# New positions for the chains' pieces of a two-layer kernel on four engines, with the transfers of SyncE left where they are

## The reference

```python
def step(h, inp):                                  # the scan: 512 channels x 16 states x 1024 positions, 4 batches
    a, bx, c = inp
    h = a * h + bx                                 # a = exp(dt * A), bx = dt * B_t * x_branch
    y = jnp.einsum('bds,bs->bd', h, c)
    return (h, y)
def step(c, xt):                                   # the recurrence over the 4 batches
    ft = jax.nn.sigmoid(xt @ wf.T + c @ uf.T + bf)
    it = jax.nn.sigmoid(xt @ wi.T + c @ ui.T + bi)
    gt = jnp.tanh(xt @ wc.T + c @ uc.T + bc)
    c = ft * c + it * gt
```

## Time and profile before

| | |
|---|---|
| time, median of 3 runs | 1270.59 us (1269.78 to 1272.22) |
| the profiled execution | 1271.65 us, of which the span is 1270.1 us |
| VectorE busy | 1159.2 us, 91% |
| TensorE busy | 1145.3 us, 90% |
| GpSimd busy | 980.9 us, 77% |
| ScalarE busy | 794.3 us, 63% |
| mean granted TensorE clock | 0.984 |

### The profile page before, as it was taken

How to read it: one execution, slowest core, us unless ns; L and a number is a source line. 1 busy time by engine, 2 the same in 40 slices (tenths; PEclk the granted TensorE clock), 3 DMA queues, 4 the chain that set the end, 5 groups by cost and what they waited for, 6 DMA issues and landing times.

```text
span 1270.1 us, 12563 instructions
## 1 busy us (share of the span) xinstructions
PE 1145.3 (90%) x3612; PEld 641.0 (50%) x3612; DVE 1159.2 (91%) x1136; ACT 794.3 (63%) x1443; POOL 980.9 (77%) x711
## 2 busy tenths in 40 slices
PE   7989678998999899998999899998999899889896
PEld 4636333654457444764457444764457444443454
DVE  3868999999999999899999999899999999999987
ACT  2256567765785677855786678855786666645522
POOL 3216886889788988989778888989778896876852
PEclk9999989999999999999999999999999999989999
DMA  8308588876878677876768588866868686989922
GB/s 280 118 15 301 188 268 286 275 233 234 278 234 291 214 275 276 296 233 235 279 219 302 207 276 286 290 230 239 281 228 292 204 279 222 306 314 351 369 84 99
DMA packets 92308, 313.87 MB, mean 247 GB/s; under 512 B 10432, under 2 KB 15680, under 8 KB 91984
## 3 DMA queue, kind: packets, MB, share of 16 engines
q1 hardware_dynamic: 89936, 306.26, 70.1%
q10 hardware_dynamic: 2304, 6.82, 1.6%
HBM read 301.73 MB, written 11.31 MB: 246 GB/s over the span
## 4 chain that ended last, share of the span: by engine, by line
PE 46%; DVE 19%; POOL 16%; ACT 9%; issue 8%; DMA 2%; SPq 0%; DVEq 0%; POOLq 0%; ACTq 0%
PE ps L874 14%; DVE ps L1691 11%; POOL arena L1914 9%; PE ps L585 5%; PE ps L808 4%; PE ps L593 3%; PE ps L631 2%; DVE arena L1697 2%; PE ps L707 2%; PE ps L720 2%; PE ps L712 2%; PE ps L735 2%; ACT arena L898 2%; ACT ps L1254 2%; PE ps L728 1%
## 5 line engine op out<-in xcount | busy, mean ns | idle before, releaser
L1914 POOL TENSOR_TENSOR arena<-arena 128x1024 f32<-128x1024 f32 x255 | 600.7, 2364 | 139.9 <-PE ps L874 115.2
L1691 DVE TENSOR_TENSOR_SCAN ps<-ps,arena 128x1024 f32<-128x1024 f32 (+1 forms) x257 | 585.9, 2280 | 29.6 <-ACT ps L1254 16.7
L874 PE MATMUL ps<-arena,identF 128*128 128x512 f32 x1024 | 484.0, 604 | 46.7 <-DVE arena L1697 29.7
L1254 ACT ACTIVATE ps<-arena,negA 128x512 f32<-128x512 f32 x512 | 332.8, 684 | 89.6 <-DVE arena L1697 83.9
L874 PEld LDWEIGHTS ps<-arena,identF 128*128 128x128 f32 x1024 | 190.8, 193 | 266.6 <-issue 209.5
L1697 DVE TENSOR_TENSOR arena<-ps,arena 128x1024 f32<-128x1024 f32 x256 | 312.0, 1219 | 5.9
L889 ACT ACTIVATE arena<-arena,rnln 128x256 f32<-128x256 f32 x118 | 61.9, 590 | 42.5 <-POOL rnln L1724 25.7
L631 PE MATMUL ps<-arena,inw 128*128 128x512 f32 x128 | 60.0, 614 | 11.7 <-ACT arena L898 9.6
L712 PE MATMUL ps<-arena,inw 128*128 128x512 f32 x128 | 62.0, 608 | 3.3 <-DVE arena L1421 3.3
L1266 ACT ACTIVATE arena<-ps 128x2 f32<-128x2 f32 x128 | 22.1, 172 | 67.9 <-DVE arena L1697 67.4
L898 ACT ACTIVATE arena<-ps,modT 128x512 f32<-128x512 f32 x43 | 51.7, 1264 | 13.7 <-PE ps L458 11.6
(11 more groups left out here) (219 smaller groups left out, 1715.7 us busy)
## 6 DMA issues: line engine op xcount, KB each, us to landing
arena<-bc_scratch SPq DMA_DIRECT2D x511, 512.0 KB, 5.0
arena<-in_x SPq DMA_DIRECT2D x16, 256.0 KB, 6.8
arena<-in_x SPq DMA_DIRECT2D x8, 512.0 KB, 8.9
xr_scratch<-arena SPq DMA_DIRECT2D x6, 512.0 KB, 6.7
px_scratch<-arena SPq DMA_DIRECT2D x6, 512.0 KB, 6.3
out_x<-arena SPq DMA_DIRECT2D x5, 512.0 KB, 2.6
arena<-bc_scratch SPq DMA_DIRECT2D x9, 256.0 KB, 3.7
woT<-in_woT SPq DMA_DIRECT2D x4, 512.0 KB, 9.4
```

The costliest lines, as they stand in the source:

```text
L874: x = pe.matmul(ps[:, Y, :], identF[:], inp[:, m % RING, q, :], start=False, stop=(i == BLOCK_STEPS - 1 and q == 1), skip_group_check=True)
L1254: x = act.activation(ps[:, 2 * (m % 2) + q, :], dt[:, kd, :], ACT.Exp, scale=negA[:, kd, 2 * i + q:2 * i + q + 1])
L1691: x = dve.tensor_tensor_scan(states, states, inp[:, m % RING, q, :].rearrange("p q t -> p (q t)"), 0.0, ALU.mult, ALU.add)
L1914: x = pool.tensor_tensor(inp[:, m % RING, :, :], u[:, kd:kd + 1, :].broadcast_to([P, 2, TH]), b_at[:, m % 3, :, :], ALU.mult)
```

## The change

All tables of `TIMES` for TensorE, ScalarE, VectorE and GpSimd get new numbers, most of them moved by a quarter of a step to two steps. The three tables of SyncE stay. No instruction is added or removed apart from ScalarE's loads of function tables, which follow the order. Lines of the difference that are spoken of below:

```diff
-    "pool_before": {"wo_gate": -5.75, "ffn_gate": -5.75, "ln1_rstd": -4.25, "ga_bias": 6.5, "op_add": (12, 12),
+    "pool_before": {"wo_gate": -7, "ffn_gate": -7, "ln1_rstd": -3.75, "ga_bias": 5.75, "op_add": (12, 12),
...
-        "first_decay": (35, 37.75), "softplus": (33.75, 34.25), "dt_copy": 37.75, "xc_silu": 28.5},
+        "first_decay": (35, 38), "softplus": (34.25, 34.25), "dt_copy": 38, "xc_silu": 27.75},
...
-        "softplus": (33.75, 33.75), "dt_copy": 41.25, "xc_silu": 28.5},
+        "first_decay": (35.75, 39), "softplus": (31.5, 34.25), "dt_copy": 39, "xc_silu": 28},
```

More of the change, by code:

```diff
@@ L67 @@
[L67 to L72, removed]
@@ L73 @@
-    "dve_second": {"ln1_stats": -13.5, "ln1_moments": -11.25, "smax": (6.75, 9), "rsum": (9, 9.5),
[3 rows of a table removed]
-    "pool_before": {"wo_gate": -5.75, "ffn_gate": -5.75, "ln1_rstd": -4.25, "ga_bias": 6.5, "op_add": (12, 12),
[L78 to L82, removed]
@@ L83 @@
-    "pool_after": {"cp_gate": -7.25, "cp_add": (5, 5), "ln4_rstd": 6.75, "f_c": 21, "i_g": 25.5, "c_new": 25.5},
[7 rows of a table added]
+        "gate_x": (12, 12.75, 17, 17.75, 21, 23.75), "gate_c": (12, 12.75, 17, 17.75, 21, 24.75), "px": (25.5, 26),
+        "om": 26},
+    "act_before": {"hn1": (-3.5, -3.5), "hB1": (-1.75, -1.75), "q0": -1.5, "k0": 1, "q1": 3.25, "exp0a": 3.75,
+        "exp0b": 3.75, "k1": 3.75, "v0": 7.25, "exp1a": 7.25, "exp1b": 7.25, "att0": 9.75, "v1": 9.75, "att1": 10.75,
+        "op_ev": (11.75, 12.75), "hn2": (14, 14), "q_scr": 17.75, "xdT": (20.25, 20.25), "ffn_ev": (21, 21),
+        "hn3": (23.5, 23.75), "hB3": (25, 25), "xc_init": (26, 26, 26.75, 26.75), "x_proj": 29,
+        "first_decay": (35, 38), "softplus": (34.25, 34.25), "dt_copy": 38, "xc_silu": 27.75},
@@ new lines @@
+    "act_second": {"hn1": (-10.25, -10.25), "hB1": (6, 6), "q0": 5.75, "k0": 5.75, "q1": 7.25, "exp0a": 7.25,
+        "exp0b": 7.25, "k1": 7.25, "v0": 9, "exp1a": 9.25, "exp1b": 9.25, "att0": 9.25, "v1": 10.25, "att1": 11.25,
+        "op_ev": (11.75, 12), "hn2": (14.25, 14.25), "q_scr": 18, "xdT": (20.25, 20.25), "ffn_ev": (20.5, 20.5),
+        "hn3": (24, 24), "hB3": (25.25, 25.25), "xc_init": (25.5, 25.5, 27.25, 27.25), "x_proj": 29.25,
+        "first_decay": (35.75, 39), "softplus": (31.5, 34.25), "dt_copy": 39, "xc_silu": 28},
@@ new lines @@
+    "act_after": {"cp_ev": (4, 5), "z_tanh": (6, 7.75, 8.5, 10), "hA": (11, 11),
+        "gate": (12.25, 15, 17.75, 20.75, 21.25, 25.25), "sigmoid": (11.5, 16.5, 17, 21.25, 22.5, 25.25),
+        "px": (26.75, 28), "hnA": (7.75, 7.75)},
+    "dve_before": {"ln1_stats": -3.75, "ln1_moments": -3.75, "smax": (3.25, 6.5), "rsum": (6.5, 8.75),
+        "ln2_stats": 13.25, "ln2_moments": 13.25, "quant": 15.5, "q_steps": (15.5, 16, 17, 17, 17, 17.75),
+        "ln3_stats": 22.25, "ln3_moments": 22.75, "pad": 23.75, "conv": (26.75, 26.75, 26.75, 28.25, 28.25, 28.25)},
@@ new lines @@
+    "dve_second": {"ln1_stats": -13.25, "ln1_moments": -10.25, "smax": (6.75, 8.5), "rsum": (8.5, 10.25),
[3 rows of a table added]
+    "pool_before": {"wo_gate": -7, "ffn_gate": -7, "ln1_rstd": -3.75, "ga_bias": 5.75, "op_add": (12, 12),
+        "ln2_rstd": 13, "n2a": 14.25, "n2b": 14.25, "q_scale": 16.25, "gb_bias": 16.25, "q_sub": 18.25,
+        "q_back": 18.25, "ffn_add": (20.25, 20.25), "ln3_rstd": 22.25, "u": (35, 38.5), "cut": (35, 38.5)},
+    "pool_second": {"ln1_rstd": -11, "ga_bias": -7.5, "op_add": (12.25, 12.25), "ln2_rstd": 12.5, "n2a": 15.25,
+        "n2b": 15.25, "q_scale": 17, "gb_bias": 17, "q_sub": 18, "q_back": 18, "ffn_add": (20, 20),
+        "ln3_rstd": 22.75, "u": (34.75, 38.75), "cut": (34.75, 38.75)},
@@ L84 @@
+    "pool_after": {"cp_gate": -8, "cp_add": (3.75, 4.5), "ln4_rstd": 6.25, "f_c": 22, "i_g": 26, "c_new": 26},
 }
```

## The result

The changed kernel took 1286.43 us in the median of 4 runs (1284.88 to 1287.46), the kernel before 1270.18 us in the median of its 4. The ratio is 1.0121, with a 95% interval of 1.0109 to 1.0133. So the change costs 16.2 us between the medians, and 14.0 us between the two profiled executions (spans of 1284.1 and 1270.1 us), where 12.5 had been forecast (1283 us).

The account below looks back on a forecast made before the run. No engine was taken as the bound by itself; some 8 us of each block are waits. The terms 11.0 - 1.7 + 3.8 - 1.7 + 4.9 - 1.7 - 2.1 gave +12.5, forecast 1283 us, range 1275 to 1293.

Parts of the forecast that it names:

- the split softplus: End of block 0: two softplus instructions ahead of decay 28 wait for dt and delay the scans, +6.0 us.
- the shorter odd blocks: Blocks 1, 3 and 5: convolution and SiLU come earlier and a table load leaves the path, -1.7 us each.
- The gate's stalls: Blocks 0, 2 and 4: GpSimd waits for `woT` ahead of input 22, making scan 22 6.5, 5.9 and 7.0 us late.
- That rival: `woT` lands sooner once GpSimd waits for it, the stalls shrink and the kernel is faster, 1264 us; chance 0.09.
- The size in blocks 2 and 4: Net delay from the gate's stall in these blocks, +3.8 and +4.9 us.
- the credit that I took off: Even blocks: the rounding's new place lets GpSimd reach input 15 about 0.65 us earlier.
- Block 0: Delay that block 0 hands on, +11.0 us: 5.0 from the gate and 6.0 from the split softplus.
- the gate's term of 5.0: Block 0: `woT` makes scan 22 6.5 us late, so `q0` of half 2 comes at 223.2, against 218.2.
- The rest costs nothing: All other moves only shift pieces among scan parts with slack, at no cost.
- the limit: A moved piece that meets a full engine costs up to its own length once a block, 0.5 to 2 us.
- Blocks 6 and 7: Block 6, without a new batch to gate, gains 2.1 us; block 7 was set to 0, with ±1.5.

Follow-up runs that it names:

- e2: The changed kernel with the first two softplus instructions of block 0 back behind decay 29; 1281.9 us.
- e3: The changed kernel with both the gate's two multiplications and the split softplus put back; 1267.9 us.
- e5: The changed kernel with SyncE's reload for blocks 0, 2 and 4 two steps earlier; 1275.8 us.
- e8: e3 with GpSimd's `f_c` also back at its old place, ahead of the gate's multiplications; 1264.0 us.
- e9: e8 with SyncE's reload one step earlier; 1265.8 us.
- e11: e8 with SiLU back behind decay 24; 1273.5 us.
- e10: e8 with `ln1_stats` back ahead of product 22; 1270.9 us.
- e1: The changed kernel with the two multiplications of `woT` and `ffnT` back behind input 22 of blocks 0, 2 and 4; 1274.1 us.
- e6_softplus_alone: The kernel before with only block 0's softplus table changed, the first two instructions ahead of decay 28; 1279.1 us.

## Why the prediction was right

The mechanism was right: the waits for `woT`, the split softplus and the shorter odd blocks are where they were forecast, and undoing the first two removed them. That the sum came within 1.5 us of the profiled difference is in part luck. Against the forecast block 0 was off by -1.0 us, blocks 2 and 4 together by +3.8, the odd blocks by +0.3, block 6 by +1.4 and block 7 by -3.0.

*The gate's stalls.* Right in mechanism and place: three waits of 11.1 to 11.6 us (9 to 12 forecast), scan 22 stalled by 6.3 and 6.7 us in blocks 2 and 4, and by 3.8 in block 0, where 6 to 7 had been forecast. The transfer didn't hurry: issued at 774.59 it landed at 784.9, 10.3 us later, and 9.1 and 9.4 us later in blocks 0 and 2. That rival is out. The table of fixed and variable time in the Trainium skill (DMA: Bandwidth & Descriptors, Anatomy of one DMA) is for a single transfer that GpSimd issues. Applied to these of SyncE, as the prediction did, it gives an estimate of 3.2 us for 512 KB; these rows disagree, as the rows before did.

*The size in blocks 2 and 4.* The terms were +3.8 and +4.9, measured +6.3 and +6.2. The step that failed is the credit that I took off: input 15 did come 0.65 us earlier, but by scan 19 the block was 0.7 us behind (see the rest, below), and SyncE's issue keeps to the row ahead of it, which came no sooner (774.59 is 13.2 us later than the earlier trace rows, as the whole block is). The transfer was 0.6 us longer in block 4 and 0.4 us in block 2, where SyncE also took 1.1 us more to issue the loads ahead of it. And behind the stall of block 2 TensorE's sums and gate products ran slowly, so that `x_proj` began 1.4 us after its input was there, and its copy waited 0.4 us for it. Together, 1.3 + 0.6 + 0.4 + 1.1 + 0.4, that is the 3.8 us by which the two terms were short.

*Block 0.* +11.0 forecast, +10.0 measured. Two errors met in the gate's term of 5.0. The transfer was issued 1.0 us sooner and took 9.1 us, not 10.7, so scan 22 was only 3.9 us late, not 6.5, and `x_proj` began 2.8 us later than before. But then it took 5.35 us in place of 3.62:

```profile
208.96 3.62 PE L707 MATMUL ps<-arena,xpw 128*33 128x512 f32 x8 [1.80 <-ACT arena L975]
```

(before; the changed kernel's is at 211.75 in the chain above.) The clock had fallen behind 3.74 us of idle time on TensorE in the stall, a cost of 1.7 us that the prediction didn't have. So SyncE issued dt 4.5 us later than before, where 5.9 had been forecast. `x_proj` takes 5.2 to 5.3 us in this block in e2, e3, e5, e8, e9 and e11 too, most of them with the gate put back, and 6.5 in e10, but 3.62 in e1, after the same 3.11 us of idle time as in e3. So the changed order as such often meets the lower clock here.

The split softplus then cost 6.5 us by e2_softplus_back, 7.7 by e6_softplus_alone, against 6.0. The load of 1.28 us is followed by the decay 0.01 us after its end (235.74 to 237.03). The Trainium skill (ScalarE: Activation LUTs, What ACT_TABLE_LOAD costs) adds about 1380 ns of draining to a load; by that price the four loads would have made the term 11.5 us, an estimate that both runs contradict.

*The odd blocks.* -1.7 three times, measured -1.4, -1.7 and -1.7. Right, and e10_stats_back and e11_silu_back show the two moves behind it.

*"The rest costs nothing".* Wrong in three places that the sum hid. The first is `f_c`: behind an input it costs 2 us in blocks 2 and 4 as soon as the gate is not early (e3_both_back against e8_fc_back, 3.9 us in the medians). In the changed kernel the scan's stall covered it, as `hn1` had no wait there. So the gate's cost against a clean order is larger than what e1_gate_back gives back.

The other two are the 1.3 us that blocks 2, 4 and 6 lose between scans 16 and 19, in every kernel with the changed tables. 0.5 us go because `ln3_stats` now stands behind the product with the gate branch (L1677), which waits 0.39 us for TensorE's sum; before, `ln3_stats` filled that wait. The other 0.8 us go at `pad`, the copy of 128 x 12 elements (L1564) that gives the convolution its first columns. It moved from ahead of product 20 to ahead of product 18. VectorE and GpSimd in block 2, before (GpSimd has nothing to do from 473.99 to 478.24):

```profile
475.26 0.16 DVE L1564 COPY arena<-arena 128x12 f32<-128x12 f32 x1
478.24 2.36 POOL L1914 TENSOR_TENSOR arena<-arena 128x1024 f32<-128x1024 f32 x1 [4.25 <-PE ps L874]
```

and in the changed kernel:

```profile
475.49 2.35 POOL L1914 TENSOR_TENSOR arena<-arena 128x1024 f32<-128x1024 f32 x1
476.85 1.02 DVE L1564 COPY arena<-arena 128x12 f32<-128x12 f32 x1
```

The copy ends 0.03 us behind GpSimd's input. So a piece can cost far more than its own length, which the prediction had set as the limit. No run has `pad` or `ln3_stats` alone put back, so what the two would give isn't measured.

*Blocks 6 and 7.* -2.1 and 0 forecast, -0.7 and -3.0 measured. Block 6 has the same loss between scans 16 and 19, from 0.6 us ahead to 0.7 behind, which is nearly all that it is short of. Of block 7's 3.0 us, 2.5 us come at one place: a product of the gate branch (L712) in the execution before and in that after, both after the same idle time:

```profile
1125.20 3.78 PE L712 MATMUL ps<-arena,inw 128*128 128x512 f32 x4 [3.27 <-DVE arena L1421]
```

```profile
1142.24 1.98 PE L712 MATMUL ps<-arena,inw 128*128 128x512 f32 x4 [3.29 <-DVE arena L1421]
```

It took 1.8 us longer in the execution before, at the lower clock, and VectorE waited 2.3 us behind it. e1_gate_back has all the moves of this block, the same product at 3.78 us after 3.28 us of idle time, and its scans gained nothing there. So this is luck of the profiled execution, and the medians, which differ by 16.2 us, fit the blocks without it.

## What to carry to other kernels

An instruction that waits for a transfer must stand behind everything that doesn't need it, and an order has to be moved for all its queues at once: here the consumer went ahead by one input while the issue on SyncE stayed, and three blocks paid a stall of 4 to 7 us. Look at what fills a wait before moving it: `f_c` was free inside the wait for `woT` and cost 2 us outside. Where two paths meet, two moves can be worth little apart and most of the gain together, so undoing them one by one overstates each.
